# Adding one column of old counts instead of twelve, and projecting finished node chunks inside the second convolution

## The reference

```python
def _sage_mean(x, src, dst, W_self, W_neigh, b, n_nodes):
    deg = jax.ops.segment_sum(jnp.ones_like(dst, dtype=x.dtype), dst, num_segments=n_nodes)
    agg = jax.ops.segment_sum(x[src], dst, num_segments=n_nodes)
    agg = agg / jnp.maximum(deg, 1.0)[:, None]
    return x @ W_self + agg @ W_neigh + b
# layer 0
h = jax.nn.relu(_sage_mean(x, ..., W_self1, W_neigh1, b1))
h = _sage_mean(h, ..., W_self2, W_neigh2, b2)
x1 = _layernorm(x + h)
# layer 1, the message of an edge
m_input = jnp.concatenate([x1[src], x1[dst], edge_attr_64], axis=-1)
h = jax.nn.relu(m_input @ W1 + b1)
messages = jax.nn.relu(h @ W2 + b2)
```

## Time and profile before

| | us |
|---|---|
| median of 3 runs | 1679.42 (1676.05 to 1679.87) |
| the profiled execution | 1675.27 |
| its span | 1673.1 |
| PE busy | 1451.8 (87%), granted clock 0.956 |
| POOL busy | 763.0 (46%) |
| VectorE busy | 754.3 (45%) |
| ScalarE busy | 667.5 (40%) |

### The profile page before, as it was taken

One profiled execution on the slowest core, in us unless ns is written; L12 is line 12 of the kernel. 1 busy time (PEld: TensorE's weight loads), 2 busy tenths in 40 slices (PEclk: granted clock), 3 DMA queues, 4 the chain that ended last, 5 costly groups with the idle time before them and its releaser, 6 DMA issues.

```text
span 1673.1 us, 30324 instructions
## 1 busy us (share of the span) xinstructions
PE 1451.8 (87%) x9336; PEld 1032.7 (62%) x9336; DVE 754.3 (45%) x2856; ACT 667.5 (40%) x1243; POOL 763.0 (46%) x806
## 2 busy tenths in 40 slices
PE   4899999999958777888989988998898889877997
PEld 3556666555556566666766766766666667654554
DVE  8799999513333222333243333333432343345445
ACT  6766666410023333443345334433443344331113
POOL 3000000000027777777777777777777777721000
PEclk9999999999978999999999998999899989988999
DMA  2000000020053333333333333333333333300001
GB/s 69 1 1 1 2 2 1 8 61 1 0 147 95 83 81 81 79 89 84 79 85 87 80 82 84 85 82 81 84 88 79 81 86 83 82 21 1 0 1 39
DMA packets 158120, 95.18 MB, mean 57 GB/s; under 512 B 119959, under 2 KB 143422, under 8 KB 158030
## 3 DMA queue, kind: packets, MB, share of 16 engines
q0 software_dynamic: 25024, 51.25, 12.0%
q1 hardware_dynamic: 133006, 42.78, 10.5%
HBM read 87.44 MB, written 6.52 MB: 56 GB/s over the span
## 4 chain that ended last, share of the span: by engine, by line
PE 31%; POOL 13%; DMA 11%; issue 9%; DVE 5%; ACT 1%; DVEq 1%; SPq 1%; POOLq 0%; ACTq 0%
POOL arena L735 13%; DMA arena<-x_w1a,idx 9%; PE ps L1167 6%; PE ps L1052 6%; PE ps L1061 5%; PE ps L1045 4%; PE ps L1041 3%; PE ps L1033 3%; PE ps L1102 2%; PE ps L1151 1%; DVE arena L2049 1%; DVE idx L2016 1%; DVEq L336 1%; DMA x_w1b<-arena 1%; DVE stats L2063 1%
## 5 line engine op out<-in xcount | busy, mean ns | idle before, releaser
L735 POOL DMA_INDIRECT arena<-x_w1a,idx x780 | 737.7, 946 | 713.3 <-issue 674.2
L1478 ACT ACTIVATE arena<-ps 88x512 f32<-88x512 f32 x196 | 116.2, 593 | 480.3 <-PE ps L1033 470.0
L1061 PEld LDWEIGHTS ps<-arena 128*128 128x128 f32 x1568 | 208.6, 196 | 111.5 <-issue 72.8
L2049 DVE TENSOR_TENSOR arena<-ps,bias_b 128x512 f32<-128x512 f32 x196 | 135.5, 691 | 208.0 <-PE ps L1052 208.0
L2044 DVE TENSOR_TENSOR arena<-win_i,late 128x96 f32<-128x96 f32 x196 | 50.8, 259 | 391.8 <-PE ps L1061 378.8
L1041 PE MATMUL ps<-ident_f,arena 128*128 128x128 f32 x784 | 130.1, 290 | 107.3 <-DMA arena<-x_w1a,idx 106.4
L1052 PE MATMUL ps<-w_c,arena 128*128 128x128 f32 x1568 | 222.6, 288 | 0.0
L1303 ACT ACTIVATE adj<-ps 128x300 f32 x392 | 171.0, 451 | 108.3 <-PE ps L800 103.8
L1045 PE MATMUL ps<-arena 88*128 88x512 f32 x392 | 208.0, 612 | 3.1 <-ACT arena L1478 3.1
L1052 PEld LDWEIGHTS ps<-w_c,arena 128*128 128x128 f32 x1568 | 205.9, 205 | 0.3
L1061 PE MATMUL ps<-arena 128*128 128x24 f32 x1568 | 197.9, 264 | 4.9 <-ACT arena L1488 1.4
(11 more groups left out here) (205 smaller groups left out, 1406.7 us busy)
## 6 DMA issues: line engine op xcount, KB each, us to landing
arena<-in_edge_attr SPq DMA_DIRECT2D x196, 128.0 KB, 2.3
arena<-x_w1a,idx POOLq DMA_INDIRECT x782
arena<-x_w1b SPq DMA_DIRECT2D x196, 12.0 KB
x_spill<-arena SPq DMA_DIRECT2D x1, 1600.0 KB, 8.6
x_w1a<-arena SPq DMA_DIRECT2D x6, 256.0 KB, 2.3
x_w1b<-arena SPq DMA_DIRECT2D x6, 256.0 KB, 2.7
arena<-x_spill SPq DMA_DIRECT2D x6, 256.0 KB, 3.4
out_x<-arena SPq DMA_DIRECT2D x3, 512.0 KB
```

The source lines that it names most:

```text
L735: pool.indirect_dma_start(out=z_e[v][:, j * D:(j + 1) * D], out_offset=None, in_=xa_d[:, :], in_offset=bass.IndirectOffsetOnAxis(ap=idx[:, ...
L1061: last = pe.matmul(ps[:, WIN_BANK[v % 2], 0:WIN], msg[:, j * P:(j + 1) * P], oh_e[v][:, j, :], start=(j == 0), stop=(j == J - 1))
L2049: dve.tensor_tensor(msg.rearrange("p (j d) -> p j d", d=D), bank(5, J), over(bias_b, J), ALU.add).then_inc(m_sum[v], 1)
```

## The change

In the counting stage, L800 adds one column of each tile's window instead of twelve: since targets are sorted, only the first node of a unit's window can have been counted by its predecessor in the stream. The two units of a stream's last block, behind which the other stream's first window may begin, keep all twelve. The test of the graph is changed to match (`tops`, `above`, `seam_a`, `seam_b`). `c1_terms` moves 386 columns, the last two both ones, and `c1_combine` takes one maximum with (0, 1) instead of two operations; `dinv` is finished once at the end.

The second convolution and the projection are one stage on the normal path. PE's `sage` for chunk c - 1 comes behind `sums_of_h(c)`; the aggregation of chunks 2 to 5 has a transposition and a projection of chunk c - 2 inside (at k = 16 and 20); ten projections (`FAST5`, m = 4 to 13) come behind the last `sage`. ScalarE does both copies of a projection. VectorE makes x1 chunk by chunk. The barrier between the stages is gone, the projection's weights go to `gamma_b` and `beta_b` early, and SyncE stores x1 behind all row stores. The general path keeps the old order.

```diff
@@ counts, PE
-                pe.matmul(ps[:, bank, 0:NT * WIN_A], ident_h[:, :], adj[:, :, bass.ds(b, WIN_A)],
+                shared = WIN_A if (i % RI, v) == (RI - 1, 2) else 1
+                window = ps[:, bank, 0:NT * WIN_A].rearrange("p (k w) -> p k w", w=WIN_A)
+                pe.matmul(window[:, :, 0:shared], ident_h[:, :], adj[:, :, bass.ds(b, shared)],
                           start=False, stop=True).then_inc(cnt_ready, 1)
@@ before the first barrier, VectorE
+            own.add(dve.scalar_tensor_tensor(out=highest, in0=half_all[:, 0:HALVES], scalar=WIN_A - 1.0,
+                                             in1=half_all[:, 1:HALVES + 1], op0=ALU.add, op1=ALU.min))
...
-            own.add(dve.tensor_reduce(off[:, 1:2], rel, mybir.AxisListType.X, ALU.max))
+            own.add(dve.tensor_tensor(above.rearrange("p (h j) -> p h j", j=J // 2),
+                                      raw_dst.rearrange("p (h j) -> p h j", j=J // 2), tops, ALU.subtract))
+            own.wait()
+            own.add(dve.tensor_reduce(off[:, 1:2], above, mybir.AxisListType.X, ALU.max))
+            own.wait()
@@ in_bounds, VectorE
-                own.add(dve.tensor_scalar(off[:, 1:2], off[:, 1:2], WIN_A - 1.0, None, ALU.subtract))
+                own.add(dve.tensor_tensor(differences[:, 0:ROUNDS], seam_a, seam_b, ALU.subtract))
+                own.wait()
+                own.add(dve.tensor_reduce(off[0:1, 6:7], differences[:, 0:ROUNDS], mybir.AxisListType.X, ALU.max))
+                own.wait()
+                own.add(dve.tensor_scalar(off[0:1, 6:7], off[0:1, 6:7], float(WIN_A), None, ALU.add))
@@ c1_combine, VectorE
+                own.add(dve.tensor_tensor(degrees_x[:, k, :], ps[:, b, 3 * D:MOV], win_i[:, 0:2], ALU.max))
                 if k < LATE_TILE:
-                    own.add(dve.tensor_scalar(inv_deg[:, k:k + 1], ps[:, b, 3 * D:3 * D + 1], 1.0, None, ALU.max))
-                    own.add(dve.tensor_scalar(dinv[:, k:k + 1], ps[:, b, 3 * D:3 * D + 1], 1.0, None, ALU.add))
                     own.wait()
-                    own.add(dve.reciprocal(inv_deg[:, k:k + 1], inv_deg[:, k:k + 1]))
+                    own.add(dve.reciprocal(inv_deg[:, k:k + 1], degrees_x[:, k, 1:2]))
@@ the merged stage
+        FAST5 = [(0, 0), (0, 1), (0, 2), (0, 3), (0, 4), (1, 0), (1, 1), (1, 2), (0, 5), (1, 3), (0, 6), (1, 4), (1, 5),
+                 (1, 6)]
+        WITHIN = 4
@@ PE
+                def turn_x1(m):
+                    h, c = FAST5[m]
+                    k0, nt = CHUNKS[c]
+                    pe.wait_ge(x1_done, c + 1)
+                    if m >= 2:
+                        pe.wait_ge(proj_ts, m - 1)
+                    for j in range(nt):
+                        last = pe.transpose(ps[:, 5 + m % 2, j * P:(j + 1) * P], xn[:, k0 + j, :], ident_f[:, :])
+                    last.then_inc(proj_t, 1)
+                def project(m):
...
+                    pe.wait_ge(proj_ts, m + 1)
+                    if m:
+                        pe.wait_ge(proj_out, m if m <= WITHIN + 1 else m - 1)
...
+                        if 2 <= c < NC - 1 and k == 16:
+                            turn_x1(c - 2)
+                        if 2 <= c < NC - 1 and k == 20:
+                            project(c - 2)
...
+                for c, (k0, nt) in enumerate(CHUNKS):
+                    sums_of_h(c)
+                    own_t(1, c, nt)
+                    if c:
+                        sage(1, c - 1, CH, fast_sums(c - 1))
+                turn_x1(WITHIN)
+                sage(1, NC - 1, CHUNKS[-1][1], fast_sums(NC - 1))
+                for m in range(WITHIN, len(FAST5)):
+                    if m + 1 < len(FAST5):
+                        turn_x1(m + 1)
+                    project(m)
@@ ScalarE
+                def projected(m):
...
+                    act.activation(fast_turned(m)[:, 0:nt * P], ps[:, 5 + m % 2, 0:nt * P], ACT.Copy).then_inc(proj_ts, 1)
+                    act.wait_ge(proj_ready, m + 1)
+                    if m >= 2:
+                        act.wait_ge(stored[FAST5[m - 2][0]][m % 2], 16 * fast_stored(m - 2, FAST5[m - 2][0]))
+                    act.activation(fast_rows(m)[:, 0:nt * D], ps[:, fast_bank(m), 0:nt * D], ACT.Copy).then_inc(proj_out, 1)
+                for c in range(NC):
+                    if 2 <= c < NC - 1:
+                        projected(c - 2)
+                    own_turned(c)
+                    if c and c < NC - 1:
+                        root(CHUNKS[c - 1][1])
+                for m in range(WITHIN, WITHIN + 3):
+                    projected(m)
+                root(CHUNKS[NC - 2][1])
+                for m in range(WITHIN + 3, WITHIN + 5):
+                    projected(m)
+                root(CHUNKS[NC - 1][1])
+                for m in range(WITHIN + 5, len(FAST5)):
+                    projected(m)
@@ VectorE
+                for c in range(NC):
+                    sums_copy(c)
+                    if c:
+                        x1_rows(c - 1)
+                    if c == 2:
+                        rows_and_places()
+                x1_rows(NC - 1)
@@ SyncE
+                for m in range(11):
+                    store_rows(m)
+                for v in range(2):
+                    features(0, v)
+                for m in range(11, len(FAST5)):
+                    store_rows(m)
+                sp.wait_ge(lin_used, 2 * NC)
+                sp.wait_ge(x1_done, NC)
+                sp.dma_start(bias_b[:, :], bcast(t["L1_gnn_b2"])).then_inc(loads[6], 16)
+                for u in range(2):
+                    sp.dma_start(w_e[u][0:R, :], t["L1_gnn_W1"][2 * D:2 * D + R, :]).then_inc(loads[6], 16)
+                sp.dma_start(x1_d[:, :].rearrange("(k p) d -> p k d", p=P), xn).then_inc(loads[5], 16)
...
+                sp.wait_ge(loads[5], 16)
```

More of the change, by code:

```diff
@@ L568, in _ @@
-            for h in range(2):
-                for u in range(2):
-                    sp.wait_ge(stored[h][u], 16 * len(stores(h, u)))
-            sp.wait_ge(loads[5], 16)
             phase_end(sp, 5)
```

291 lines of the change are left out of this document (197 added, 94 removed).

## The result

The changed kernel takes 1656.16 us (median of 4 runs, 1654.62 to 1660.81), the kernel before on the same chip 1679.34 us (4 runs, 1676.05 to 1679.87). The medians are 23.2 us apart; the ratio is 0.9877, 95% interval 0.9863 to 0.9892, which makes 20.7 us (18.1 to 23.0). The forecast was 1654.7, a gain of 24.7.

The account below looks back on a forecast made before the run. PE and VectorE were taken to be nearly full in the counting stage, POOL's gathers to set the edge loop. Gains of 20.7 us (counting) and 4.0 (merged stage) make 24.7, from 1679.4 to 1654.7, range 1643 to 1667.

Parts of the forecast that it names:

- rounds 0 and 1: Counting stage before 100 us: of VectorE's 15.8 us of waits for PE, 3 us stay (0 to 8).
- end lag: End of counting stage: PE's lag behind VectorE falls from 4.7 to about 1.8 us, 2.9 us gained.
- rounds 2 to 6: Later counting stage: VectorE becomes the bound, a round takes 38.1 us against 40.2; 1 of 6.9 us of waits stays.
- late degrees near 287 us: Sign at the counting stage's end: the late degrees on PE start near 287 us instead of 308.
- vanishing waits: Sign in the counting stage: VectorE's waits for PE on L795 nearly vanish.
- one sign of being wrong: PE's granted clock under 1.00 before the second convolution's first aggregation (S) would show the prediction wrong.
- First barrier: Before the first barrier: two added VectorE operations and a wait lose 1.6 us (0 to 1.8).
- rival (a): Counting stage: ScalarE or hand-overs, not PE's columns, held VectorE in rounds 0 and 1; gain 12 us, 1667; chance 0.13.
- Part 2: Projection inside the second convolution: barrier at S + 159.3 instead of S + 163.2, 4 us gained (bounds -5 to 10).
- The narrow addition: Counting stage, L800 at 25 columns instead of 300: 0.10 us of PE saved per unit (0.04 to 0.14).
- Rival (c): Merged stage's tail: all its steps run at 1.2 GHz, 7.2 us longer; total gain 17.5, 1662; chance 0.12.
- Rival (d): Counting stage: PE, less busy, loses its clock; slower than before, 1697 if 100 us run at the lower clock; chance 0.06.

Follow-up runs that it names:

- experiment 3: Changed kernel with x products in rounds 0 and 1 replaced by short ones: 1651.67; ScalarE's two x copies one tile wide: 1655.51; product burst split in two: 1654.44.
- the last one of experiment 5: Changed kernel with the projection tail overlapped, x1 stored in one piece, late-degree products five at a time between the 24 terms, x products in one burst: 1645.12, ratio 0.9812.
- the one with short copies: Changed kernel with ScalarE's copies of the turned chunk and own product one tile wide instead of four, x values wrong: 1655.51, ratio 0.9884.
- experiment 4, first kernel: Changed kernel with the 1600 KB x1 store cut into 7 chunk stores ahead of the last row stores: 1655.95, ratio 0.9866.
- second: Changed kernel with x1 stored by chunks, next turned copy ahead of current rows copy, earlier root of chunk 5 and reordered projections: 1643.82, ratio 0.982.

## Why the prediction was right, point by point

The total was right to 1.5 us, and no rival came true as a whole. That it was so near is partly luck: rounds 0 and 1 gave 9 us less than forecast and the end lag 1.3 less, and what made up for it are 3.3 us more in rounds 2 to 6, which are the mechanism, and about 2 us each up to S and behind it, which are mostly these two executions. Of my signs, the late degrees near 287 us and the vanishing waits did not come (294.49, 12.2 us), and one sign of being wrong did by its letter: PE's clock fell to 0.50 before S, outside the counting stage, as it had in the kernel before. The terms one by one:

- **First barrier:** 1.7 us lost, 1.6 said. Checks in round 2: 0.36 us more (from the first of them to the next block, 3.45 to 3.81), 0.5 said.
- **Rounds 0 and 1: the term that failed.** I let 3 of 15.8 us of VectorE's waits stand, and 12.2 stood. In these two rounds the outcome is that of rival (a), but its cause is at most the smaller part: by experiment 3, 7.4 of the 12.2 us go with TensorE's products, and splitting their burst of 1.9 us without taking any away removes 2.9. What the other 4.8 us are is open; TensorE waits for ScalarE 6.0 us in 20 pieces from 20 to 100 us, 3.4 us in 14 before. I had averaged PE over the stretch (70.7 of 80 us), and an average doesn't show that in a burst VectorE runs out of free buffers, though it has four. The wait's longest piece, 2.3 us, was a sign for it.
- **Rounds 2 to 6:** 9.9 us gained, 6.6 said (5.9 of waits, 1.2 less 0.5). The round itself was forecast to the tenth, 38.1 us, and came at 38.0. Five rounds of 40.2 less 38.1 make 10.5; I summed the listed waits and overlapping operations instead, and they miss the short gaps. Where a stage repeats, the difference of two periods is the better term.
- **End lag:** from 4.7 to 3.1 us, 1.6 gained, 2.9 said.
- **Up to S:** 1.9 us more, not foreseen. Before, PE's clock fell twice between the late degrees and S (24 terms in 5.60 us, the last 75 in 14.20), in this execution after only once (4.12 and 14.20). The sibling kernels with one short fall need 27.8 to 28.3 us there as well, also the narrow addition alone (28.2) and the wide one in the merged kernel (28.0). The 1.9 us are the second fall of the one trace of before, and no run shows that the change has a part in them.
- **Part 2:** 5.9 us from S to the 21st gather, 4.0 said. The stations stood where they were put: POOL's start S + 145.0 (144.5), last rows copy S + 147.3 (147), store issued S + 149.7 (149), barrier S + 158.4 (159.3), one pause. The store landed in 8.0 us where I gave it 9.8. POOL's second pause (1.41 us), which I had let out of the sum, vanished here, but it stands at 1.5 us in three of the six executions with this code. The 4.0 us that I forecast are what four of the six show.
- **The narrow addition** cost 0.03 us in PE's queue, as L853's 26 ns had said. The Trainium skill's page TensorE: Matmul & The Clock Gate, section LDWEIGHTS, divides the 128 columns of a load by 1.2 GHz, and the estimate by it is 107 ns for the load alone; by this row the trace does not agree.
- **Rival (c)** was partly true: behind the pause of 2.24 us two products ran at the lower clock, about 0.4 and 0.6 us longer than at full clock, not the whole tail; in two executions with this tail one more group followed. Rival (d) did not come: the clock stayed at 1.00 in the counting stage with PE 93% busy.
- "Whatever PE does" is the edge loop's length, I wrote; the last one of experiment 5 and the one with short copies show that this holds only while PE has its clock.

## What to carry to other kernels

Cost a faster engine by the period of the stage that it leaves, and look for bursts on it: a mean share of busy time says nothing of a queue that one long piece of work blocks while the engine that feeds it runs out of free buffers. Where several conditions end in one unbroken run, write each as a time of its own and take the latest: an edit to one of them alone wins only the distance to the next, and two small ones together can win more than their sum. Before a difference of 1 or 2 us at a point of a trace is given to a change, look at the same stretch in several executions of the same code, with the granted clock beside it: here it varied by 2 us from execution to execution. In a chain of copy, product, copy on two engines, put the next item's first copy ahead of this item's last one.

## What the hardware did that I had not expected

- In ten of twelve traces the granted clock was 0.50 to 0.65 in the 2.5 us behind 125 one-column matmuls in a row (3.3 us), though PE shows as busy there (2.79 of 3 us); in the other two it fell to 0.50 some 12 us behind them. In two traces with the same matmuls five at a time between products of 386 columns it was 1.00 all the way to S.
- A matmul of 25 columns with its own 128 x 128 weights takes up 0.03 us of PE's queue although its record is 0.20 us long.
- One store of 1600 KB took 8.0 us from issue to landing. In seven pieces between row stores of 256 KB it did not keep POOL from starting at S + 137.6, but ScalarE waited 2.3 us (experiment 4, first kernel) and 3.2 us (second) for a row store at the end.
- At the start of the edge loop PE had the lower clock for 5 to 6 us in some executions and for over 10 us in others of the same code. In the nine executions that store x1 in one piece POOL's second pause, 1.3 to 1.5 us, came with the five longer stretches and with none of the four shorter ones.
